# Causal attention: remainders of two neighbouring P tiles in one GpSimd instruction, the four-block tile through PSUM to VectorE

## The reference

```python
q = heads(x @ Wq + bq); k = heads(x @ Wk + bk); v = heads(x @ Wv + bv)
bias = alibi_bidirectional_bias(H, S, x.dtype)   # even heads of the kernel: keys up to the query; odd: keys from the query on
scores = jnp.einsum('bhqd,bhkd->bhqk', q, k) * (1.0 / np.sqrt(hd)) + bias[None]
attn = jax.nn.softmax(scores, axis=-1)
out = jnp.einsum('bhqk,bhkd->bhqd', attn, v)
```

## Time and profile before

| | |
|---|---|
| median of three runs | 3126.95 us (3123.92 to 3128.47) |
| the profiled execution | 3123.28 us |
| its span | 3121.1 us |
| causal stage, GpSimd's first remainder to the last P·V | 415.1 to 993.7 us |
| cross stage's remainders on GpSimd | 1189.1 to 2098.7 us (start of the last) |
| TensorE, VectorE, ScalarE, GpSimd busy, whole span | 84%, 74%, 56%, 60% |
| mean granted TensorE clock | 0.935 |

### The profile page before, as it was taken

One profiled execution on the slowest core, in us unless ns is written; L12 is line 12 of the kernel. 1 busy time (PEld: TensorE's weight loads), 2 busy tenths in 40 slices (PEclk: granted clock), 3 DMA queues, 4 the chain that ended last, 5 costly groups with the idle time before them and its releaser, 6 DMA issues. The chain is left out here.

```text
span 3121.1 us, 77095 instructions
## 1 busy us (share of the span) xinstructions
PE 2634.2 (84%) x24119; PEld 1431.1 (46%) x24119; DVE 2318.2 (74%) x4525; ACT 1762.4 (56%) x3255; POOL 1874.1 (60%) x1424
## 2 busy tenths in 40 slices
PE   7999478888886869999999999980999899703999
PEld 3555235555554534555555555550444344301444
DVE  8888667777775767888888888867333467697776
ACT  3444257777775435666666666654233477696333
POOL 3444479999997317999999999996100144300000
PEclk9999779999998988999999999995999999856999
DMA  8999724444445662222122131115644588797332
GB/s 305 336 334 342 267 96 134 136 126 131 135 133 169 235 202 60 53 75 66 51 80 62 49 98 50 47 54 172 214 153 158 200 278 281 258 415 282 110 126 81
DMA packets 320920, 511.28 MB, mean 164 GB/s; under 512 B 35669, under 2 KB 155221, under 8 KB 320810
## 3 DMA queue, kind: packets, MB, share of 16 engines
q1 hardware_dynamic: 317674, 503.65, 48.3%
q0 software_dynamic: 1952, 6.29, 0.6%
q10 hardware_dynamic: 1184, 0.01, 0.0%
HBM read 270.95 MB, written 194.28 MB: 149 GB/s over the span
## 5 line engine op out<-in xcount | busy, mean ns | idle before, releaser
L1102 POOL TENSOR_TENSOR cross_plo<-cross_p 128x1024 f16<-128x1024 f32 x448 | 906.6, 2058 | 73.4 <-ACT cross_p L940 69.7
L940 ACT ACTIVATE cross_p<-cross_st 128x512 f32<-128x512 f32 x1024 | 556.2, 595 | 289.1 <-PE cross_st L874 289.0
L1015 DVE CUSTOM_DVE_ANT_0 cross_junk<-cross_sc,rows 128x1024 bf16<-128x1024 f32 x512 | 619.0, 1219 | 110.5 <-PE cross_sc L835 98.2
L1102 POOL TENSOR_TENSOR self_plo<-self_p 128x1024 f16<-128x1024 f32 (+7 forms) x512 | 577.0, 1165 | 19.1 <-ACT self_p L940 18.8
L940 ACT ACTIVATE self_p<-self_st,self_strip 128x512 f32<-128x512 f32 (+3 forms) x768 | 415.3, 582 | 148.0 <-PE self_st L872 116.8
L1015 DVE CUSTOM_DVE_ANT_0 self_junk<-self_sc,self_strip 128x1024 bf16<-128x1024 f32 (+7 forms) x512 | 371.1, 752 | 140.8 <-PE self_sc L835 136.0
L869 PE MATMUL cross_st<-cross_qa,cross_ka 97*128 97x512 f16 x1024 | 390.4, 381 | 2.5 <-ACT cross_p L940 1.7
L874 PE MATMUL cross_st<-rows,idbig 128*128 128x512 f16 x1024 | 389.9, 381 | 0.0
L835 PE MATMUL cross_sc<-cross_ka,cross_qa 96*128 96x512 f16 x1024 | 311.3, 386 | 22.3 <-DMA cross_ka<-scr_k_hi 16.7
L897 PEld LDWEIGHTS cross_o<-cross_vh,cross_p 128*128 128x128 bf16 x4096 | 270.1, 97 | 75.0 <-issue 21.7
L897 PE MATMUL cross_o<-cross_vh,cross_p 128*128 128x65 f16 x4096 | 297.4, 191 | 4.6 <-POOL cross_plo L1102 4.2
(11 more groups left out here) (254 smaller groups left out, 5710.3 us busy)
## 6 DMA issues: line engine op xcount, KB each, us to landing
self_strip<-self_strips SPq DMA_DIRECT2D x68, 516.0 KB, 3.2
scr_gate<-gt_y SPq DMA_DIRECT2D x96, 256.0 KB, 2.1
v_w<-scr_gate SPq DMA_DIRECT2D x96, 256.0 KB, 4.1
scr_h<-v_w SPq DMA_DIRECT2D x96, 256.0 KB, 4.0
j_h<-scr_h SPq DMA_DIRECT2D x48, 512.0 KB, 9.6
d_o<-scr_o SPq DMA_DIRECT2D x9, 1536.0 KB
scr_up<-v_y SPq DMA_DIRECT2D x48, 256.0 KB, 4.3
j_u<-scr_up SPq DMA_DIRECT2D x24, 512.0 KB, 12.0
```

What stands on the lines that cost most here:

```text
L940: nc.scalar.activation(p32[u % NPR][:, q0:q1], stp[cc % 2][:, 0:q1 - q0], ACT.Exp, bias=bias, scale=SM).then_inc(expd, 1)
L1015: nc.vector.tensor_tensor_reduce(junk[slot % 2][:, 0:w], sc[slot % 2][:, 0:w], bias, 1.0, -3e38, ALU.add, ALU.max, qmax[n % 2][:, qt:qt + ...
L1102: nc.gpsimd.tensor_tensor(plo[u % NPR][:, q], p32[u % NPR][:, q], high[:, q], ALU.subtract).then_inc(lo_g, 1)
```

## The change

The leads and the number of buffers become local: in the causal stage SLEAD is 21 and ELEAD 8, with 8 pairs of P buffers (16 units); in the cross stage they stay at 19, 6 and 4 pairs (8 units). Two neighbouring units lie side by side in one tile (`spot`): 8 + 1, 7 + 2, 6 + 3 and 5 + 4 blocks, always 1152 columns. In the causal stage GpSimd makes the remainder of the first three pairs of a head with one instruction each, as soon as the second unit's exponential is done (`lows_of`), and that of the five-block unit alone.

The four-block unit, the last of a head, goes another way. One slot of the row-wise scores shrinks to 512 columns (its units are never wider), and the PSUM bank that this frees becomes `whole`. The key-wise scores of the four-block unit go there. ScalarE makes the exponential twice: once in BF16 into the P tile in SBUF, and once in f32 in place in PSUM. VectorE subtracts the first from the second and writes the remainder. TensorE waits with the next such unit until that subtraction is done. In the cross stage each unit's instructions stay what they were.

```diff
-SLEAD = 19
-ELEAD = 6
-NPR = 8
+PAIR = 2
+        SLEAD, ELEAD, NPP = (21, 8, 8) if causal else (19, 6, 4)
+        NPR = PAIR * NPP
+        PW = S + P if causal else PAIR * S
-        p32 = [sb(f"p32_{j}", [P, S], F32) for j in range(NPR)]
-        plo = [sb(f"plo{j}", [P, S], F16) for j in range(NPR)]
+        p32 = [sb(f"p32_{j}", [P, PW], F32) for j in range(NPP)]
+        plo = [sb(f"plo{j}", [P, PW], F16) for j in range(NPP)]
-        sc = [kit.ps(f"{name}_sc{j}", [P, S]) for j in range(2)]
+        sc = [kit.ps(f"{name}_sc{j}", [P, GT if causal and j else S]) for j in range(2)]
+        if causal:
+            whole, high_made = kit.ps(f"{name}_whole", [P, GT]), sem("high_made")
         def on_vector(u):
-            return not causal and u % UH == 4
+            return u % UH == (UH - 1 if causal else 4)
+        def spot(u):
+            return u // PAIR % NPP, 0 if u % PAIR == 0 else (width(u - 1) if causal else S)
+        def high_of(u):
+            j, b = spot(u)
+            if causal and on_vector(u):
+                return p32[j][:, b:b + width(u) // 2].bitcast(BF16)
+            return p32[j][:, b:b + width(u)].bitcast(BF16).rearrange("p (q h) -> p q h", h=2)[:, :, 1]
+        def lows_of(u):
+            j, b = spot(u)
+            if on_vector(u) or causal and u % PAIR == 0 and not on_vector(u + 1):
+                return None
+            if causal and u % PAIR == 1 and not on_vector(u - 1):
+                return j, 0, b + width(u)
+            return j, b, b + width(u)
...
             # TensorE, key_scores
+                    if causal and on_vector(u) and (not isinstance(i, int) or i > 0 or u >= UH):
+                        pe.wait_ge(lo_v, i * LV + lows_by(u, True) - 1)
-                        w, out = q1 - q0, stp[cc % 2]
+                        w, out = q1 - q0, whole if causal and on_vector(u) else stp[cc % 2]
             # TensorE, values
+                    if causal and on_vector(u):
+                        pe.wait_ge(high_made, i * LV + lows_by(u, True))
             # ScalarE, exps
+                        if causal and on_vector(u):
+                            nc.scalar.activation(high_of(u), whole[:], ACT.Exp, bias=bias, scale=SM).then_inc(high_made, 1)
+                            nc.scalar.activation(whole[:], whole[:], ACT.Exp, bias=bias, scale=SM).then_inc(expd, 1)
+                            continue
             # VectorE, low
+                    if causal:
+                        dve.wait_ge(high_made, i * LV + lows_by(u, True))
                     dve.wait_ge(expd, i * CS + chunks_by(u) + 2)
-                    nc.vector.tensor_tensor(plo[u % NPR][:, q], p32[u % NPR][:, q], high[:, q], ALU.subtract).then_inc(lo_v, 1)
+                    nc.vector.tensor_tensor(plo[j][:, q], whole[:] if causal else p32[j][:, q], high_of(u), ALU.subtract).then_inc(lo_v, 1)
             # GpSimd, low
-                    if on_vector(u):
+                    if lows_of(u) is None:
                         return
                     pool.wait_ge(expd, i * CS + chunks_by(u) + 2)
-                    nc.gpsimd.tensor_tensor(plo[u % NPR][:, q], p32[u % NPR][:, q], high[:, q], ALU.subtract).then_inc(lo_g, 1)
+                    j, a, z = lows_of(u)
+                    high = p32[j][:, a:z].bitcast(BF16).rearrange("p (q h) -> p q h", h=2)[:, :, 1]
+                    nc.gpsimd.tensor_tensor(plo[j][:, a:z], p32[j][:, a:z], high, ALU.subtract).then_inc(lo_g, 1)
```

More of the change, by code:

```diff
@@ L675, in on_vector, with width, lows_by @@
         def on_vector(u):
-            return not causal and u % UH == 4
-        def lows_before(u, vector):
-            return sum(on_vector(m) == vector for m in range(u))
-        LV, LG = lows_before(HB * UH, True), lows_before(HB * UH, False)
+            return u % UH == (UH - 1 if causal else 4)
+        def width(u):
+            n, k, kt = keys_of(u)
+            a, z = query_range(n, kt)
+            return z - a
+        def spot(u):
[12 more added lines that the diff above has]
+            return j, b, b + width(u)
+        def lows_by(u, vector):
+            if vector:
+                return sum(on_vector(m) for m in range(u + 1))
+            return sum(lows_of(m) is not None for m in range(u + 1)) + (lows_of(u) is None)
+        LV, LG = lows_by(HB * UH - 1, True), sum(lows_of(m) is not None for m in range(HB * UH))
         def within(last, u):
@@ L884, in values @@
                     pe.wait_ge(expd, i * CS + chunks_by(u) + 2)
+                    if causal and on_vector(u):
+                        pe.wait_ge(high_made, i * LV + lows_by(u, True))
                     if on_vector(u):
-                        pe.wait_ge(lo_v, i * LV + lows_before(u, True) + 1)
+                        pe.wait_ge(lo_v, i * LV + lows_by(u, True))
                     else:
-                        pe.wait_ge(lo_g, i * LG + lows_before(u, False) + 1)
+                        pe.wait_ge(lo_g, i * LG + lows_by(u, False))
                     a, z = query_range(n, kt)
-                    high = p32[u % NPR][:].bitcast(BF16).rearrange("p (q h) -> p q h", h=2)[:, :, 1]
+                    j, b = spot(u)
+                    high, rest = high_of(u), plo[j][:, b:b + width(u)]
                     for qt in range(a // P, z // P):
-                        q = slice(qt * P, (qt + 1) * P)
+                        q = slice(qt * P - a, qt * P - a + P)
                         out = ob[qt // 4]
@@ L897, in values @@
                         nc.tensor.matmul(out[:, qt % 4, :], high[:, q], vh[n % NQK][:, kt, :], start=first, stop=False, skip_group_check=True)
-                        mm = nc.tensor.matmul(out[:, qt % 4, 0:HD + 1], plo[u % NPR][:, q], vh[n % NQK][:, kt, 0:HD + 1],
+                        mm = nc.tensor.matmul(out[:, qt % 4, 0:HD + 1], rest[:, q], vh[n % NQK][:, kt, 0:HD + 1],
                                               start=False, stop=last_kt, skip_group_check=True)
@@ L939, in exps @@
                         bias = strip[n % NQK][:, S + kt:S + kt + 1] if causal else 0.0
-                        nc.scalar.activation(p32[u % NPR][:, q0:q1], stp[cc % 2][:, 0:q1 - q0], ACT.Exp,
+                        if causal and on_vector(u):
+                            nc.scalar.activation(high_of(u), whole[:], ACT.Exp, bias=bias, scale=SM).then_inc(high_made, 1)
+                            nc.scalar.activation(whole[:], whole[:], ACT.Exp, bias=bias, scale=SM).then_inc(expd, 1)
+                            continue
+                        nc.scalar.activation(p32[j][:, b + q0 - a:b + q1 - a], stp[cc % 2][:, 0:q1 - q0], ACT.Exp,
                                              bias=bias, scale=SM).then_inc(expd, 1)
@@ L1025, in low @@
                         return
+                    if causal:
+                        dve.wait_ge(high_made, i * LV + lows_by(u, True))
                     dve.wait_ge(expd, i * CS + chunks_by(u) + 2)
-                    q = slice(*query_range(n, kt))
-                    high = p32[u % NPR][:].bitcast(BF16).rearrange("p (q h) -> p q h", h=2)[:, :, 1]
-                    nc.vector.tensor_tensor(plo[u % NPR][:, q], p32[u % NPR][:, q], high[:, q], ALU.subtract).then_inc(lo_v, 1)
+                    j, b = spot(u)
+                    q = slice(b, b + width(u))
+                    nc.vector.tensor_tensor(plo[j][:, q], whole[:] if causal else p32[j][:, q], high_of(u), ALU.subtract).then_inc(lo_v, 1)
                 def gather(i, n):
@@ L1095, in low @@
                 def low(i, u):
-                    n, at, kt = keys_of(u)
-                    if on_vector(u):
+                    if lows_of(u) is None:
                         return
                     pool.wait_ge(expd, i * CS + chunks_by(u) + 2)
-                    q = slice(*query_range(n, kt))
-                    high = p32[u % NPR][:].bitcast(BF16).rearrange("p (q h) -> p q h", h=2)[:, :, 1]
-                    nc.gpsimd.tensor_tensor(plo[u % NPR][:, q], p32[u % NPR][:, q], high[:, q], ALU.subtract).then_inc(lo_g, 1)
+                    j, a, z = lows_of(u)
+                    high = p32[j][:, a:z].bitcast(BF16).rearrange("p (q h) -> p q h", h=2)[:, :, 1]
+                    nc.gpsimd.tensor_tensor(plo[j][:, a:z], p32[j][:, a:z], high, ALU.subtract).then_inc(lo_g, 1)
                 def prologue():
```

## The result

The changed kernel takes 3193.5 us (median of four, 3189.7 to 3200.1) against 3127.7: a ratio of 1.0205, 95% interval 1.0182 to 1.0229. It is 66 us slower; the forecast was 3204 us. The profiled execution took 3192.84 us, its span 3190.7, 69.6 us over that of before.

The account below looks back on a forecast made before the run. The causal stage was taken to be bound by TensorE, VectorE and ScalarE in turn, not GpSimd. 10.25 us a head against 9.0 over 63 turns gave 79 us more on 3123.3, forecast 3204 us, range 3098 to 3232.

Parts of the forecast that it names:

- It is full, but it holds nobody: Causal stage before: GpSimd is busy 577.0 of 578.6 us, yet nobody waits for it, so cutting its work gains nothing.
- P·V to scores of step 1: Start of a head, from step 0's P·V; step k has the head's k-th P·V product of eight: 0.45 us.
- scores to maximum: From step 1's row-wise scores (5 blocks) on TensorE to their maximum on VectorE: 0.65 us.
- VectorE's row: VectorE without a gap: 640 and 512 maxima, new subtraction, division, 1024 maximum until step 5's scores go out: 4.17 us.
- scores of step 5 to those of step 7: Seven-block scores to their maximum, 0.77 us, then that maximum until the next scores go out: 1.93 us in all.
- the turn: Step 7, head's end: scores, matmul, two exponential passes, accumulator copy, gather, next P·V: 3.16 us against 2.40 before.
- the 0.1 given back: Taken off the 10.36 us a head because the division would run with GpSimd idle a quarter of the time.
- The four-block tile: Two 512-column exponentials on ScalarE, 0.58 us each, and a VectorE subtraction, 0.61: 0.6 us more on each engine, not hidden.
- The clump: VectorE's 4.17 us row: TensorE stands about 1 us at step 5's scores, waiting for step 3's 1024 maximum.
- Start and end: nothing: Causal stage: two more units ahead at the start, as much less at the end, so no change in time.
- GpSimd was the bound: First rival: the head falls with GpSimd's work to 8.4 us, kernel 3087 us; chance 0.21.
- The clump is absorbed: Rival: only the turn at step 7 counts, division and subtraction slip behind other work; 9.5 us a head, 3157 us; chance 0.17.

Follow-up runs that it names:

- pool_light: The kernel before with GpSimd's causal remainder made for only the first 128 columns of each unit: 3117.9 us, ratio 0.9974.
- after_one_exp: The changed kernel without the first (BF16) of the four-block tile's two exponentials: 3156.7 us, ratio 1.0121.
- after_sub0: The changed kernel with VectorE's subtraction moved from step 2 to step 0 of a head: 3184.1 us, ratio 1.0195.
- after_div0: The changed kernel with the reciprocal and division moved from step 2 to step 0 of a head: 3140.2 us, ratio 1.0055.
- whole_19_6: The changed kernel with the leads of before (19, 6), everything else kept: 3184.5 us, ratio 1.0188.
- pairs_psum: The changed kernel with all four pairs on GpSimd, no four-block tile through PSUM, leads 21 and 8, gathered accumulator in PSUM: 3115.7 us, ratio 0.9974.
- before_psum: The kernel before with the gathered accumulator in PSUM, one row-wise score slot shrunk to 512 columns: 3114.3 us, ratio 0.9964.
- pairs_19_6: The changed kernel with all four pairs on GpSimd, no tile through PSUM, old leads (19, 6): 3176.4 us, ratio 1.0157.
- after_singles: The changed kernel with GpSimd's pairing taken back, seven instructions a head, one for each unit: 3288.8 us, ratio 1.0516.

## Why the prediction was right, step by step

**The bound.** "It is full, but it holds nobody" was right on the load (pool_light) and wrong on the instruction. The empty list of waiters shows waits on semaphores only. GpSimd held VectorE's division for 0.28 us a head on average, and their collision cost the head 0.16.

**The walk.** Set against the head of after, term by term (forecast, then measured): P·V to scores of step 1 0.45, 0.46; scores to maximum 0.65, 0.65; VectorE's row 4.17, 4.03; scores of step 5 to those of step 7 1.93, 1.92; the turn 3.16, 2.90. Sum 10.36, 9.96; with the 0.1 given back 10.25, against a mean of 10.06. Two terms were mis-sized. The division was priced at 0.92 with its reciprocal and took 0.78. The copy to the gather was priced at 0.49 from a head in which the gather waited for a maximum (in the earlier trace rows it starts at 601.22, as the 896-column maximum from 600.20 ends) and took 0.31; gather to P·V took 0.62 for 0.71. The excess over before, 1.04 us by the mean, was forecast as 1.25: over the stage 62 us (the last P·V 67.1 us later, less the first one's 5.1) for 79. The 5.1 us at the start and 2.5 behind the stage, which the sum had at nothing, brought the time nearer to the forecast by luck.

**The four-block tile.** A pass of 0.58 and a subtraction of 0.61 were right (575.49 to 576.07, 570.08 to 570.68), the write into PSUM included, which was a guess between 0.4 and 0.7: 0.65 by its duration for 0.69 into SBUF. That both are on the path was right for the pass: 0.49 us by after_one_exp. It was wrong for the subtraction as I told it: after_sub0 gives back 0.12 us. The length of the row came out right all the same, because work that fills a wait makes the same row as work that adds to one: with the subtraction out of its way the division lasts 1.09 us in place of 0.48 (after_sub0). That part is luck.

**The leads.** "The clump" is real (0.84 us of idle TensorE, expected about 1), but the part of it that a choice of step decides is the division beside a GpSimd instruction. Taking it out of the row gave 0.84 us (after_div0).

**Start and end: nothing** was wrong by 5.1 us: two more units of scores and of exponentials stand in front of the first P·V. That it is the leads fits whole_19_6, which has the old ones and starts at 420.5. The expected saving at the end appears (the last but one head takes 8.47 us), but it did so before as well (8.38 and 8.30).

**GpSimd's work.** Three pairs of 2.11, 2.29 and 2.11 us and one of 1.25 make 7.76 us, within 7.5 to 8.0. The second pair is longer by 0.18, as it meets the division, which pairs_psum removes. The same is the excess of the 1024 form in the earlier trace rows, which I had left unexplained: it stands behind the division, and in before_psum it is gone (1.89 us). The contention of the two engines I had weighed only for what it costs GpSimd; it costs VectorE more, 0.28 us a head before and 1.1 in pairs_19_6. The Trainium skill, "GPSIMD Engine Reference", section 1, states contention with VectorE instructions that have two SBUF inputs; the runs agree (1.55 us for the division in pairs_19_6, 0.42 with one of its inputs in PSUM).

**The rivals.** "GpSimd was the bound" falls with pool_light. "The clump is absorbed" falls for after, where TensorE still waits 0.84 us at the clump. The busy times that the first rival was reckoned from were misread by a little: by the earlier trace rows a head has 6.7 us of VectorE and 7.6 of TensorE, not 6.9 and 7.4. Nothing in the sum hangs on it.

## What to carry to other kernels

A step on VectorE with two SBUF operands and a GpSimd instruction can exclude each other (here the division, and the cross stage's subtraction of 1024 columns), and neither the waits nor the idle times show it: compare an instruction's shortest and mean duration, and look at what GpSimd was in when it lasted long. Merging GpSimd instructions saves their fixed cost and lengthens that wait, so first put one operand in PSUM or move the step to where GpSimd idles. Here the operand was worth 0.36% by itself; pairing alone cost 1.6%, and with both cures it brought about 0.3%. An engine that is 100% busy may cost next to nothing by its load, until the others get faster than it.

## What the runs showed of the hardware that I had not expected

- A two-operand SBUF division of 256 columns took 0.42 us alone and up to 1.98 us behind one GpSimd instruction (pairs_19_6); it ended 0.28 us after the end of the GpSimd instruction that it met, whether that lasted 1.04 us (before), 1.68 (after_singles) or 2.11 (pairs_19_6). Where that end was only 0.11 us away, it took its 0.42 us (every fourth head of after). With one operand in PSUM it took 0.42 us.
- The GpSimd instruction behind the division lasts 0.18 us longer for it (2.29 for 2.11, pairs_19_6).
- The cross stage of before has the same in its 64 subtractions of 1024 columns on VectorE: each ended 1.08 us after the end of the GpSimd instruction that it met, and the GpSimd instruction behind it took 2.88 us for 1.89.
- TensorE's granted clock stood at its lower level (0.50, 1.2 GHz) and at its upper (1.00, 2.4 GHz) within three microseconds of one head in after_singles, where TensorE idled 1.62 us once a head on average in front of the scores of step 5 (mean clock 0.85 from 450 to 950 us); in after, where that idle was 0.89 us on average, the mean was 1.00.
